# Cross-attention stage of a decoder kernel: a second PSUM bank for the turned probabilities, three banks for the rest, and another order of VectorE's work in a slot

## The reference, cut to what matters

```python
xn = _rmsnorm(x, rms_scale)
mn = _rmsnorm(mem_seq, rms_scale)
q = einsum('BTD,NDH->BTNH', xn, q_w)          # 4 heads of 128
k, v = einsum('BSD,cKDH->cBSKH', mn, kv_w)    # one key and value head
q, k = rope(q) * 128 ** -0.5, rope(k)
probs = softmax(where(mem_mask, q @ k, MASK_FILL))
enc = probs @ v
x = x + einsum('BTNH,NHD->BTD', enc, out_w)
```

## Time and profile before

| | us |
|---|---|
| median of 3 runs | 3125.34 (3122.75 to 3126.17) |
| the profiled execution, its own time | 3125.27 |
| its span, first to last instruction | 3123.5 |
| TensorE busy | 3007.7 (96%) |
| VectorE busy | 1942.9 (62%) |
| ScalarE busy | 1304.6 (42%) |
| GpSimd busy | 912.8 (29%) |

### The profile page before, as it was taken

The page is one execution under the profiler, slowest core; times in us unless marked ns, Lnnn a source line. Parts: engine busy times, 40 slices in busy tenths (PEclk is TensorE's granted clock), DMA queues, the critical chain, the costliest instruction groups (busy, mean ns, idle before and its releaser), DMA issues.

```text
span 3123.5 us, 39398 instructions
## 1 busy us (share of the span) xinstructions
PE 3007.7 (96%) x14628; PEld 2515.5 (81%) x14628; DVE 1942.9 (62%) x4095; ACT 1304.6 (42%) x2511; POOL 912.8 (29%) x681
## 2 busy tenths in 40 slices
PE   7999999999979999999999999999999999999999
PEld 6888888888867777777777777888888888888887
DVE  6888888888767777777777766324332233332355
ACT  4444343434356666666666653112121121112243
POOL 0101010111367677767676750000000000000144
PEclk9999999999989999999999999999999999999999
DMA  7777777878532433243324331211121111211386
GB/s 206 190 208 209 212 202 206 211 203 206 184 95 86 120 97 108 82 123 96 109 82 117 88 122 68 68 41 55 49 59 41 41 49 54 60 27 44 131 288 227
DMA packets 319631, 380.07 MB, mean 122 GB/s; under 512 B 15312, under 2 KB 175056, under 8 KB 319440
## 3 DMA queue, kind: packets, MB, share of 16 engines
q1 hardware_dynamic: 319440, 377.56, 41.8%
HBM read 232.80 MB, written 130.02 MB: 116 GB/s over the span
## 4 chain that ended last, share of the span: by engine, by line
PE 82%; DVE 7%; issue 5%; ACT 3%; POOL 1%; SPq 1%; DMA 0%; DVEq 0%
PE c_p L132 11%; PE c_p L131 11%; PE c_p L130 11%; PE a_p L131 5%; PE a_p L130 5%; PE a_p L132 5%; PE b_n L130 3%; PE b_n L132 3%; PE b_n L131 3%; PE b_t L1712 2%; PE d_p L131 2%; PE d_p L130 2%; PE d_p L132 2%; PE a_p L1012 2%; PE a_r L954 2%
## 5 line engine op out<-in xcount | busy, mean ns | idle before, releaser
L1305 POOL TENSOR_SCALAR b_soft<-b_soft,b_one_in_sum 128x512 f32<-128x512 f32 x256 | 400.5, 1566 | 259.0 <-DVE b_one_in_sum L1509 259.0
L1972 ACT ACTIVATE c_gate<-c_p,c_bias 128x512 f32<-128x512 f32 x180 | 124.2, 690 | 682.6 <-PE c_p L132 682.6
L2002 DVE TENSOR_TENSOR c_gate<-c_gate,c_gate 128x512 f32<-128x512 f32 x64 | 44.2, 691 | 502.7 <-ACT c_gate L1972 502.7
L1528 DVE TENSOR_TENSOR b_p_lo<-b_t,b_p_hi 128x512 fp32r<-128x512 f32 x256 | 174.4, 681 | 192.0 <-ACT b_p_hi L1377 190.4
L351 POOL TENSOR_TENSOR kept_scale<-c_ln_ve,minus_half 128x4 f32<-128x4 f32 x16 | 16.1, 1009 | 880.0 <-DVE c_ln_ve L343 880.0
L1368 ACT ACTIVATE b_soft<-b_soft,b_minus_top 128x512 f32<-128x512 f32 x256 | 186.0, 726 | 165.8 <-DVE b_minus_top L1520 159.4
L1377 ACT ACTIVATE b_p_hi<-b_t 128x512 fp32r<-128x512 f32 x256 | 151.9, 593 | 147.5 <-PE b_t L1712 146.3
L351 POOL TENSOR_TENSOR a_ln_sc<-a_ln_ve,minus_half 128x4 f32<-128x4 f32 x16 | 16.3, 1017 | 635.8 <-DVE a_ln_ve L343 635.8
L648 ACT ACTIVATE a_elu<-a_p 128x512 f32<-128x512 f32 x128 | 75.5, 589 | 286.7 <-PE a_p L132 286.7
L1712 PE MATMUL b_t<-ident,b_soft 128*128 128x128 f32 x1024 | 157.3, 276 | 33.1 <-DVE b_p_lo L1528 33.0
L1712 PEld LDWEIGHTS b_t<-ident,b_soft 128*128 128x128 f32 x1024 | 124.1, 142 | 66.0 <-DVE b_p_lo L1528 41.8
(11 more groups left out here) (295 smaller groups left out, 9610.8 us busy)
## 6 DMA issues: line engine op xcount, KB each, us to landing
a_mem_moving<-in_ctx SPq DMA_DIRECT2D x64, 256.0 KB, 5.2
a_mem_turned<-in_ctx SPq DMA_DIRECT2D x16, 1024.0 KB, 9.2
x<-a_mem_turned SPq DMA_DIRECT2D x16, 1024.0 KB, 7.8
a_res<-in_x SPq DMA_DIRECT2D x16, 1024.0 KB, 6.3
x<-a_res SPq DMA_DIRECT2D x16, 1024.0 KB, 5.3
b_memT_f<-x SPq DMA_DIRECT2D x16, 1024.0 KB, 5.9
b_x<-x SPq DMA_DIRECT2D x16, 1024.0 KB, 5.5
b_res<-x SPq DMA_DIRECT2D x16, 1024.0 KB, 5.5
```

The source lines that it names most:

```text
L1305: pool.tensor_scalar(soft[:, at, :], soft[:, at, :], one_in_sum[:, at:at + 1], None, ALU.mult).then_inc(p_norm.sem, p_norm.unit)
L1528: dve.tensor_tensor(part.low, pT_bank[:, :].rearrange("p (i s) -> p i s", i=T), part.high_f32(), ALU.subtract).then_inc(p_lo.sem, p_lo.unit)
L1972: act.activation(gate[j % 2][i][:, :], gating.banks[(3 * j + i) % 6][:, :], ACT.Tanh if g == "c" else ACT.Sigmoid, bias=added[:, i, j:j + ...
```

## The change

It has five parts.

1. The turned probabilities get two banks, used in turn (`pT_banks[j % 2]`), so `turn_p(j)` waits for `p_low(j-2)` instead of `p_low(j-1)`.
2. The rota has three banks and eleven jobs. The places for tokens are gone; in step 0 the turned tokens take the places of the output. The turned keys now get the bank of output tile 1 (event `x2_sb`).
3. VectorE's order in a slot is: one over the sum, masked minimum, low half, then squares (`tokens_turned`) and the memory's low halves (slots 14 and 15, which move ahead of the other work of the slot). Before, it was squares, low half, masked minimum.
4. Moved by slots: `keys(0)` and its rounding `values_high(0)` from slot 1 to 3; the third head's query work from slots 3, 4 and 5 (VectorE, ScalarE, GpSimd) to 1, 2 and 3. In the last two steps the weights of stage c are turned in other slots and banks, with waits of their own.
5. In stage a the load of batch 1 is issued ahead of the first memory's loads, and in step 0 VectorE takes the statistics of batch 1 in one piece behind the low halves of Wq.

```diff
             def sync(sp):
                 first_loads(sp)
-                load_memory(sp, 0)
...
                     if following(new, B):
                         load(sp, new.b + 1)
+                    if old is None:
+                        load_memory(sp, 0)
...
-            KV, TOKENS, OUT, KT = 0, 2, 3, 2 + 2 * T
+            KV, OUT, KT = 0, 2, 2 + T
...
-            jobs = [(k_rope, 2, 0), (k_rope, 6, 0)]
-            for t in range(T):
-                jobs += [(xT_lo, t, 0), (x2_sb, t, 2)]
+            jobs = [(k_rope, 2, 0), (k_rope, 6, 0)] + [(x2_sb, t, 2) for t in range(T)]
...
-            pT_bank = self.banks(held, "b_t", 1)[0]
-            turns = Rota(self.banks(held, "b_n", 4), jobs, B)
+            pT_banks = self.banks(held, "b_t", 2)
+            turns = Rota(self.banks(held, "b_n", 3), jobs, B)
...
-                        if new and new.b >= 1 and 5 <= j <= 8:
-                            tokens_turned(j - 5)
+                        if old and j < J - 2:
+                            masked(old.b, j + 2)
+                        if new and j >= J - 2:
+                            masked(new.b, j - J + 2)
                         if old and j >= 1:
                             p_low(old.b, j - 1)
                         if fin and j == 0:
                             p_low(fin.b, J - 1)
-                        if old and j < J - 2:
-                            masked(old.b, j + 2)
-                        if new and j >= J - 2:
-                            masked(new.b, j - J + 2)
+                        if new and new.b >= 1 and 5 <= j <= 8:
+                            tokens_turned(j - 5)
+                        if after and j >= 14:
+                            memory_low(after, j - 12)
...
-                            if j == 1:
+                            if j == 3:
                                 keys(0)
...
                     def turn_p(j):
-                        if free := earlier(p_lo, old.b, j, 1):
+                        if free := earlier(p_lo, old.b, j, 2):
                             pe.wait_ge(*free)
...
                     def turn_keys():
                         bank = bank_of(KT)
+                        if s == 0:
+                            pe.wait_ge(xT_lo.sem, xT_lo.upto(0))
```

More of the change, by code:

```diff
@@ L802, in step @@
                         outer_taps(0, 3)
-                    if after:
+                    if after and old:
                         self.norm_tile(dve, N, after, x, 0)
@@ L818, in step @@
                         weight_low(WQ, 2)
+                    if after and old is None:
+                        for t in range(T):
+                            self.norm_tile(dve, N, after, x, t)
+                        self.norm_variance(dve, N, after)
                     if after:
@@ L1247, in gate_weight, with gate_bank, out_job @@
             def gate_weight(s, j):
-                at = {(0, 0): (0, 0), (0, 1): (0, 2), (0, 5): (1, 0), (0, 6): (1, 2), (0, 8): (2, 0), (0, 9): (2, 2), (0, 14): (3, 0), (0, 15): (3, 2),
+                at = {(0, 0): (0, 0), (0, 1): (0, 2), (0, 8): (1, 0), (0, 9): (1, 2), (0, 10): (2, 0), (0, 11): (2, 2), (0, 14): (3, 0), (0, 15): (3, 2),
                       (1, 0): (4, 0), (1, 2): (4, 2), (1, 4): (5, 0), (1, 6): (5, 2)}.get((s - B, j))
-                return at and [(at[0], at[1] + c, turns.bank(s, 2 * c)) for c in range(2)]
+                return at and [(at[0], at[1] + c, gate_bank(s, at[0], c)) for c in range(2)]
+            def gate_bank(s, i, c):
+                if i >= 4:
+                    return (turns.bank(s, OUT + 2), pT_banks[1])[c]
+                return turns.bank(s, (KV if i == 0 else KT) + c)
+            def out_job(s, t):
+                return OUT + (t if s <= B else t % 2)
             def earlier(event, b, k, back):
@@ L1401, in tokens_high @@
                         act.wait_ge(x_turned.sem, x_turned.upto(new.b, c))
-                        source = turns.bank(s, TOKENS + 2 * c)[:, :] if new.b == 0 else nT_f[:, c, :]
+                        source = turns.bank(s, OUT + c)[:, :] if new.b == 0 else nT_f[:, c, :]
                         if c == 0 and new.b >= 1:
@@ L1527, in p_low @@
                         part = p[h % 2][:, :, t * P:(t + 1) * P]
-                        dve.tensor_tensor(part.low, pT_bank[:, :].rearrange("p (i s) -> p i s", i=T), part.high_f32(),
+                        dve.tensor_tensor(part.low, pT_banks[j % 2][:, :].rearrange("p (i s) -> p i s", i=T), part.high_f32(),
                                           ALU.subtract).then_inc(p_lo.sem, p_lo.unit)
@@ L1552, in tokens_low @@
                         dve.wait_ge(xT_hi.sem, xT_hi.upto(new.b, c))
-                        dve.tensor_tensor(nT.low[:, c, :], turns.bank(s, TOKENS + 2 * c)[:, :], nT[:, c, :].high_f32(), ALU.subtract).then_inc(xT_lo.sem, xT_lo.unit)
+                        dve.tensor_tensor(nT.low[:, c, :], turns.bank(s, OUT + c)[:, :], nT[:, c, :].high_f32(), ALU.subtract).then_inc(xT_lo.sem, xT_lo.unit)
                     def keys(g):
@@ L1739, in turn_x @@
                     def turn_x(c):
-                        bank = bank_of(TOKENS + 2 * c)
+                        bank = bank_of(OUT + c)
                         if c == 0:
@@ L1745, in out @@
                     def out(t):
-                        bank = bank_of(OUT + 2 * t)
+                        if s <= B or t < 2:
+                            bank = bank_of(OUT + t)
+                        else:
+                            bank = turns.bank(s, out_job(s, t))
+                            pe.wait_ge(x2_sb.sem, x2_sb.upto(fin.b, t - 2))
+                        if s == B and t == 1:
+                            pe.wait_ge(gates.split_lo.sem, gates.split_lo.upto(0))
+                        if s == B + 1 and t == 0:
+                            pe.wait_ge(gates.split_lo.sem, gates.split_lo.upto(3))
                         if t == 0:
```

22 lines of the change are left out of this document (12 added, 10 removed).

## The result

| | us |
|---|---|
| before, median of 4 runs | 3124.07 (3122.75 to 3126.17) |
| changed, median of 4 runs | 3028.80 (3028.35 to 3029.96) |
| ratio | 0.9695, 95% interval 0.9678 to 0.9712 |
| forecast | 3054, range 3036 to 3084 |

The profiled execution took 3028.35 us, 96.9 less than the one before.

The account below looks back on a forecast made before the run. TensorE was taken to bound the kernel, busy 3007.7 of 3123.5 us. Terms: 58.2 - 8.4 + 8.3 + 6 + 2 + 5 = 71.1 us off 3125.3, so 3054 us, range 3036 to 3084.

Parts of the forecast that it names:

- The keys' wait: Stage b, before the keys are turned: TensorE's wait for the bank's last owner goes, 14 x 2.54 = 35.6 us.
- the low half in slot 2: Stage b, slot 2: the wait for the turned probabilities' low half goes with a second bank, 14 x 1.22 = 17.1 us.
- the memory's low half: Stage b, slot 15: it moves ahead of one addition on VectorE, so its 0.39 us wait goes, 5.5 us.
- no steady wait in slot 9: Denies the first rival: the wait moves to the queries, 2 to 2.6 us in slot 9; 3089 us, chance 0.14.
- none of a whole step: Denies the third rival: the loop paces slots 5 to 15, 7.7 us a step; about 3162 us, chance 0.04.
- I take 0.6 us a step: Stage b: lateness from VectorE's new order, a loss of 8.4 us, between nothing and 2.5 us a step.
- by these durations it is about even: Slots 5 to 9: 2 to 3 us of lateness stands against nearly 3 us of slack at the queries' fourth part.
- The clock's five falls: Stage b: five falls to half clock behind the 2.54 us waits go, 8.3 us gained.
- Steps 0 to 2: Stage b's opening: step 0 costs 1.5 us, step 1 gains 3.5, so 2 together; ends -2 and 8.
- The loop of 4.5 us a slot: Slots 5 to 8: the chain from one exponential to the next takes some 4.5 us against TensorE's 3.87 us slot.
- Start and end: Start: waits for batch 1 and Wq go, 6 us gained; last two steps: waits for probabilities' low halves shrink, 5 us.
- the second rival: Stage b, keys: VectorE and GpSimd block each other, 14 x 1.5 = 21 us, giving 3075 us; chance 0.08.

## Why the prediction was right and wrong

**The mechanism was right.** The keys' wait, the low half in slot 2 and the memory's low half were what TensorE waited for in each step, all three went, and no other wait took their place in these steps. Each can be brought back by its own part of the change: the keys' wait by its event, the low half's by one bank with the rotation in slot 1, the memory's by the old place. The profile shows what was asked for: no wait at the turned keys, steps all alike, the clock at 1.00 from 930 to 1740 us. None of the rivals came: no steady wait in slot 9, none of a whole step. Steps of 57.2 us are shorter than the 58 to 59 given.

**What failed: "14 x 2.54", "14 x 1.22" and "0.39", each priced by its idle time.** The step gained 4.91 us, not 4.15. By the distances of the turnings in the two traces the slot with the keys went from 7.06 to 4.31 us (2.75 for 2.54 shown), slots 2, 3 and 4 from 3.94, 2.68 and 3.95 to 2.56, 2.56 and 3.87 (1.58 for 1.22; slot 2 alone 1.38), and slot 0 from 4.63 to 4.00 (0.63 for 0.39). The prediction's own rows held this: from 1209.30 the row of the turning is 0.66 long. Some 0.16 us of each wait lie under the row of the matmul before it, and a wait delays the slots behind it a little too. Two experiments show it for themselves, the memory's low half (0.48 shown, 0.73 paid) and one bank (nothing shown, 0.69 paid). Over 13 steps that is 9.9 us.

**What failed: "I take 0.6 us a step".** The lateness of the new order is real, 1.5 us over four slots and not the 2 to 3 worked out (the squares start 4.11 us apart in the changed kernel, not 4.5), but it never reaches TensorE: the kernel with the old order has the same 57.22 us. The step that failed is "by these durations it is about even". There were 2.9 us to spend before the fourth part of the queries, so the lower end, nothing, was the value to take. 13 x 0.6 = 7.8 us. With the 9.9 above this is the whole miss of the steady steps.

**The second bank.** The prediction gave it the 1.22 us and named the rotation's move in the same breath. The two are alternatives: the bank alone leaves 0.03 us a step, the move alone 0.69. What only the bank brings is the end, where the trace gains 6.9 us for the 5 taken.

**The clock's five falls** came out as forecast, 8.3 us in the 13 steps. What was underrated is the other side: a wait of 4.4 us in place of 2.54 brings a fall each time, in 14 of 14.

**Steps 0 to 2.** Step 0 cost 1.7 us for the 1.5 taken. Step 1 was forecast at 3.5 and gave, up to its turned keys, 12.2 (49.17 to 36.96 us); of this the wait at the keys is 5.4, those for probabilities shrank from 6.4 to 3.3 before the turned keys, and one for the low half of the memory from 2.5 to 1.5; that one stands at 883.65 us, just ahead of the stretch of the earlier trace rows, so the 11.8 us read there are not all of the waits. The rest is the granted clock: before, it was half over most of 901 to 918 us, in the changed kernel in shorter pieces, 0.82 against 0.91 in the mean of 866 to 922 us, which is 5 us of full clock. The prediction had no term for that, nor for the memory's wait. The loop of 4.5 us a slot was right in place, but its price, 3.0 us at the queries, fell into step 2, which gained 0.5 us (64.25 to 63.77) where 3.6 were forecast.

**Start and end** are 6.9 each in the two traces for 6 and 5. The direct tests of the start give less, 0 to 2 us at the end of the program, and two executions of the same code differ by 3.2 us behind the last turned keys. Both terms are no better known than that. Much of what the start gains is given back in falls of the clock in the last two steps, which came with some executions and not with others; what decides that stays open.

**The rule against the change.** Beside GpSimd's multiplication by a scalar a VectorE addition with two SBUF inputs again took 0.68 us:

```profile
1109.51 1.56 POOL L1316 TENSOR_SCALAR b_soft<-b_soft,b_one_in_sum 128x512 f32<-128x512 f32 x1 [0.72 <-DVE b_one_in_sum L1520]
1110.56 0.68 DVE L1603 TENSOR_TENSOR b_rope<-b_rope 128x512 f32<-128x512 f32 x1
```

and beside its two-input subtraction the keys' multiplication took 0.86 where its twin takes 0.41:

```profile
1116.46 1.29 POOL L1328 TENSOR_TENSOR b_q_lo<-b_rope,b_q_hi 128x512 fp32r<-128x512 f32 x1
1117.17 0.86 DVE L1578 TENSOR_TENSOR b_k_f<-b_k_scaled,b_cos_k 128x256 f32<-128x256 f32 x1
...
1120.62 0.41 DVE L1578 TENSOR_TENSOR b_k_f<-b_k_scaled,b_cos_k 128x256 f32<-128x256 f32 x1
```

So the second rival's blocking is there, half a microsecond once a step, and the slack took it. The Trainium skill ("SBUF — State Buffer", "Who interferes with whom") has it for any GpSimd instruction that reads SBUF; as before, the first of these rows does not agree.

**The range** was too narrow at its low end: it stood on the idle times as an upper bound of the gain, which they are not.

## What to carry to other kernels

Price a wait of TensorE by the distance between two starts, with and without it, and not by the idle time in front of it; a first row that is longer than its twins (0.66 for 0.60) marks a wait that shows no idle time at all. Before an order costs something, its lateness has to use up the slack at the one instruction that needs the result, so find that instruction and read both times. In a rota of banks look for owners that no longer write: one such wait carried more than half of this gain, and kept beside the rest of the change, it cost all of it (3130.0 us).

## What the runs showed of the hardware

A wait of TensorE costs 0.16 to 0.25 us more than its idle time in the profile (1.38 for 1.22, 2.75 for 2.54, 0.63 for 0.39, 0.73 for 0.48), and waits of 0.14 and 0.19 us are not shown. The granted clock fell to half at each of 14 waits of 4.4 us, behind five of 14 waits of 2.54 us, and at the waits of 1.8 us and less in the last steps in two traced executions of the changed kernel and not in the third; a short fall costs 1.6 to 1.7 us, and at the waits of 4.4 us 1.7 to 3.4 us of full clock were lost. That is the 3.2 us by which the traced executions differ behind their last turned keys (1322.2 against 1325.4 and 1325.5).
